# A VectorE shuffle for the pair swap of the rotary embedding, dummy products on TensorE, and units moved by tables

## The chip, the cores and the metric

One NeuronCore of a Trainium2 chip runs the kernel. The metric is the device time of one execution in microseconds (us), of which three were taken. The engines are TensorE (PE, with its weight loads apart as PEld), VectorE (DVE), ScalarE (ACT), GpSimd (POOL) and SyncE (SP), which issues most of the DMAs.

## The reference

The input `x` is (4, 1024, 256). It is normalised over its last axis, goes through a causal attention with 16 heads of 64 and through a mixture of 32 experts, and both results are added to `x`:

```python
xn = _layernorm(x)
q, k, v = (split_heads(xn @ W) for W in (Wq, Wk, Wv))
q, k = apply_rope(q), apply_rope(k)
attn = softmax(where(causal, q @ k.T * d**-0.5, -inf))
x = x + (attn @ v).merged @ Wo + bo + _L0_ffn_ref(xn, ...)
```

`apply_rope` turns neighbouring pairs of features. With `x1` the even and `x2` the odd feature, the even output is `x1*cos - x2*sin` and the odd one `x1*sin + x2*cos`. So every feature needs its neighbour's value. The expert part softmaxes gate logits over the tokens, takes the 8 best tokens per expert, merges them, runs two layers of 257x1024 and 1025x256 per expert, and adds the result back to those tokens.

## The kernel before, in words

All five engines run programs written out by hand, with semaphores between them. The work is a row of stages `(P, g)`: `P` is one of 32 steps (4 batches times 8 pairs of heads) and `g` is 0 to 5. Two stages `(-1, 4)` and `(-1, 5)` stand ahead of them. In stage `(P, g)` TensorE does, in this order:

- the scores of two key chunks of pair `P` (`scores`, L1448 to L1460), into the PSUM tiles `t_pA` and `t_pB`;
- the products from which the row maxima of pair `P + 1` are taken (`maximum`, L1472 and L1479), into `t_pC` and `t_pA`;
- one projection of a coming pair (`fill`), into the PSUM bank `t_pF`: q or k (L1525) at g = 0, 1, 4, 5, v (L1508) at g = 2, 3. A fill may start when the bank was read, that is when all earlier `cos_done` and `fill_read` are there;
- `turn_maxima` (L1536) at g = 1 and 4; then a `unit` of the opening, or slots of the expert layers, or output products;
- the products of the exponentials with v (`values`, L1550) into `t_pO`, and the sums (L1559).

A q or k fill is turned with features on the partitions, so a pair of features lies on two neighbouring partitions. Five steps follow it: ScalarE copies the bank to `t_raw` (`evict`, L861); SyncE issues two DMAs that copy even rows of `t_raw` to odd rows of `t_swap` and the reverse (L653, L622 for the first four); VectorE multiplies the bank with the cosines (`rope`, L1132, which also waits for `raw_done`); GpSimd multiplies `t_swap` with the sines (L737) and adds both (L740). Then ScalarE rounds the result to `t_HI` (`high`, L871) and VectorE takes the rest, `t_LO` (`low`, L1122). ScalarE may overwrite `t_raw` only when the DMAs of the last swap have landed:

```python
r = ROPE[f]
if r > EARLY:
    swap_ready(act, r - 1)
act.activation(raw_of(r), bank, ACT.Copy).then_inc(raw_done, 1)
```

Each engine goes through the stages with an order of its own. ScalarE: exponentials (L839), `high`, `evict`, weight rounding, units. VectorE: row maxima (`TENSOR_REDUCE`, L1098), `shift` (L1112), `low`, `combine` (L1105), `rope`, the reciprocal and normalisation of outputs (L1082, L1090), weight remainders (L1309), units, statistics. GpSimd: the `rope` of the stage before, then the additions of the exponentials into `t_acc` (L758 to L762).

In the opening (`P` up to 5) the batches 1 to 3 are made ready between the attention stages: `spread` (L1205) and `statistics` take sums, `variance(2)` and `moments(2)` make mean and scale of these batches, `normalise` on ScalarE (L934) applies them, the unit `x` transposes them (L1644), ScalarE and VectorE split them (L946, L1251), and the unit `logit` makes gate logits. The tables `STATISTICS_AT`, `NORM_AT` and `UNITS_AT` say in which stage each of these stands. A unit uses the upper banks of `t_pC` and `t_pB`, and the second score chunk of the next stage waits until VectorE has read them.

`warm(n)` (L1693) multiplies the identity with itself into `t_pO`, and nothing reads the result. It stands at two places before the first fill, with 16 and 4 products.

Of the kernel before, what the change touches and what calls it, by code (L numbers as in the profile page):

```python
# [30 lines left out]
P128 = 128  # L31
# [99 lines left out]
def parts_of(P, g):  # L131
# [4 lines left out]
UNITS_AT = {(0, 5): ("logit", 0), (1, 5): ("x", 1, 0), (2, 1): ("x", 1, 1), (2, 2): ("logit", 1), (2, 3): ("x", 2, 0),  # L136
            (3, 1): ("x", 2, 1), (3, 2): ("logit", 2), (3, 3): ("x", 3, 0), (4, 1): ("x", 3, 1), (4, 2): ("logit", 3),
# [4 lines left out]
STATISTICS_AT = {(0, 2): [(1, 0)], (0, 3): [(1, 1)], (0, 4): [(2, 0)], (0, 5): [(2, 1)], (1, 0): [(3, 0)], (1, 1): [(3, 1)]}  # L142
NORM_AT = {(1, 4): [(1, 0, (0, 1, 2, 3))], (1, 5): [(1, 1, (4, 5))], (2, 0): [(1, 1, (6, 7))], (2, 1): [(2, 0, (0, 1))],
           (2, 2): [(2, 0, (2, 3))], (2, 4): [(2, 1, (4, 5))], (2, 5): [(2, 1, (6, 7))], (3, 1): [(3, 0, (0, 1))],
           (3, 2): [(3, 0, (2, 3))], (3, 4): [(3, 1, (4, 5))], (3, 5): [(3, 1, (6, 7))]}
# [40 lines left out]
def attend_block(nc, x, wq, wk, wv, wo, bo, gate_w, gate_b, w1, w2, rot_cos, rot_sin, out):  # L186
# [17 lines left out]
    with ExitStack() as ctx:  # L204
# [64 lines left out]
        raw = sb("t_raw", [P128, BANK])  # L269
# [45 lines left out]
        def raw_of(r):  # L315
            return PT[:, r // 2, r % 2, :] if r < EARLY else raw[:, :]

# [18 lines left out]
        raw_done = sem("t_raw_done")  # L336
        swapped = [sem(f"t_swapped{i}") for i in range(2)]
# [35 lines left out]
        first_swapped = [sem(f"t_first_swapped{r}") for r in range(EARLY)]  # L373
# [107 lines left out]

        def swap_ready(engine, r):
            if r < EARLY:
                engine.wait_ge(first_swapped[r], 32)
            else:
                engine.wait_ge(swapped[r % 2], ((r - EARLY) // 2 + 1) * 32)
# [5 lines left out]
        def _(sp):  # L492
# [145 lines left out]
            for s, (P, g) in enumerate(STAGES):  # L638
# [91 lines left out]
        def _(pool):  # L730
            def rope(f):
# [4 lines left out]
                swap_ready(pool, r)  # L736
# [84 lines left out]
        def _(act):  # L821
            def exp(P, c, j):
# [5 lines left out]
                if n < PTS:  # L828
                    for r in range(2 * (n % 2), 2 * (n % 2) + 2):
                        if n < 2:  # L830
                            act.wait_ge(first_swapped[r], 32)
                        else:
                            act.wait_ge(first_turned[r], 1)
                else:
                    m = n - PTS
                    act.wait_ge(pv_done, m + 1)
                    P0, (c0, j0) = m // len(CHUNKS), CHUNKS[m % len(CHUNKS)]
                    act.wait_ge(acc_done, ACC_OPS[P0, c0, j0 if j0 else 1])
                act.activation(PT[:, n % PTS, :, 0:w], bank[:, :, 0:w], ACT.Exp, scale=SCALE).then_inc(exp_done, 1)  # L839

            def evict(f):

                n = FILL[f]
                bank = fill_bank(f)
                act.wait_ge(proj_done, n + 1)
                if f[0] == "v":
                    unit, t = f[1:]
                    if t < 4:
                        if unit >= 2:
                            act.wait_ge(pv_done, chunk_index(2 * unit - 3, 1, 3) + 1)  # L850
                        dst = V0[:, unit % 2, t:t + 2, :]
                    else:
                        if unit >= 1:
                            act.wait_ge(pv_done, chunk_index(2 * unit - 1, 1, 7) + 1)
                        dst = V1[:, t - 4:t - 2, :]
                    act.activation(dst, bank.rearrange("p (t n) -> p t n", t=2), ACT.Copy).then_inc(fill_read, 1)
                else:
                    r = ROPE[f]
                    if r > EARLY:
                        swap_ready(act, r - 1)  # L860
                    act.activation(raw_of(r), bank, ACT.Copy).then_inc(raw_done, 1)  # L861
# [140 lines left out]
            evict(("q", 0, 1))  # L1002
            evict(("k", 0, 1))
# [11 lines left out]
            for s, (P, g) in enumerate(STAGES):  # L1015
# [28 lines left out]
                if fill_of(P, g):  # L1044
                    evict(fill_of(P, g))
# [15 lines left out]
                if (P, g) == (1, 3):  # L1061
                    root(2)
# [15 lines left out]
        def _(dve):  # L1078
# [46 lines left out]
            def rope(f):  # L1125
# [166 lines left out]
            def first_sine(f):  # L1292
# [3 lines left out]
                swap_ready(dve, r)  # L1296
# [523 lines left out]
```

## Time and profile before

| what | value |
|---|---|
| median of 3 runs | 1391.26 us (1390.22 to 1393.01) |
| the profiled execution's own time | 1394.52 us |
| its span, first to last instruction | 1392.7 us |
| mean granted TensorE clock | 0.984 |
| TensorE matmul busy | 1326.8 us, 95% |
| VectorE busy | 876.9 us, 63% |
| ScalarE busy | 640.9 us, 46% |
| GpSimd busy | 976.6 us, 70% |
| moved by DMA | 188.88 MB |

An engine's busy time is a sum over stretches with different limits. Since TensorE stands at 95%, the table is read by its other 5%: 65.9 us of the span in which it ran nothing. The clock is a share of 2.4 GHz, and 0.50 in a stretch is the lower level of 1.2 GHz.

### The profile page before, as it was taken

To read this page: it belongs to the slowest core of one execution; us is meant where nothing else is said; L and a number is where in the kernel's file an instruction comes from. 1 tells how busy PE (TensorE), PEld (TensorE's weight loads), DVE (VectorE), ACT (ScalarE), POOL (GpSimd) and SP (SyncE) were. 2 spreads that over 40 slices of the span, in tenths; PEclk is the share of its full clock that TensorE was granted. 3 is DMA by queue.
4 is the path that set the end of the run, shared out by engine and by line. 5 is a ranking of instruction groups with operands and counts; after the bars stand their busy time and mean duration, and the time that the engine had idled before them with its cause. 6 is when DMAs were issued, how large, how long until landed. Compare 5 with 4: busy or idle time off the path is not lost.

```text
span 1392.7 us, 31589 instructions
## 1 busy us (share of the span) xinstructions
PE 1326.8 (95%) x11676; PEld 870.7 (63%) x11676; DVE 876.9 (63%) x1185; ACT 640.9 (46%) x969; POOL 976.6 (70%) x661
## 2 busy tenths in 40 slices
PE   6898999999899999999899999999999999999998
PEld 5565666655565555556667676666656776666656
DVE  5687667865555666556555666665757666665753
ACT  3445655543453344435433434544444434455542
POOL 2676667865665666558666777887879777888954
PEclk9898999999999999999999999999999999999999
DMA  5322333487678667774552221212232121222111
GB/s 179 116 73 86 140 138 123 169 287 249 221 257 298 217 219 240 270 245 154 150 167 77 89 85 62 78 63 78 92 108 89 63 77 62 77 66 81 61 58 62
DMA packets 122753, 188.88 MB, mean 136 GB/s; under 512 B 29616, under 2 KB 57808, under 8 KB 122608
## 3 DMA queue, kind: packets, MB, share of 16 engines
q1 hardware_dynamic: 92176, 112.51, 24.6%
q10 hardware_dynamic: 30384, 74.23, 15.5%
q8 instruction: 101, 1.65, 0.5%
q14 instruction: 44, 0.36, 0.1%
q0 software_dynamic: 48, 0.13, 0.1%
HBM read 130.71 MB, written 22.54 MB: 110 GB/s over the span
## 4 chain that ended last, share of the span: by engine, by line
PE 71%; DMA 10%; DVE 7%; POOL 3%; issue 3%; ACT 3%; SPq 2%; ACTq 0%; DVEq 0%; POOLq 0%
PE t_pO L1550 15%; PE t_pF L1525 11%; PE t_pA L1448 8%; PE t_pB L1448 6%; PE t_pF L1508 5%; DMA t_swap<-t_raw 4%; PE t_pA L1472 3%; PE t_pC L1472 3%; DMA r_s<-t_rcomp 2%; PE t_pC L1599 2%; PE t_pB L1599 2%; PE t_pA L1453 2%; PE t_pC L1559 2%; PE t_pB L1453 2%; POOL t_acc L762 2%
## 5 line engine op out<-in xcount | busy, mean ns | idle before, releaser
L762 POOL TENSOR_TENSOR t_acc<-t_acc,t_PT 128x1024 f32<-128x1024 f32 (+3 forms) x256 | 433.2, 1692 | 153.9 <-ACT t_PT L839 133.4
L737 POOL TENSOR_TENSOR t_swap<-t_swap,t_sin 128x512 f32<-128x512 f32 x124 | 169.9, 1370 | 199.8 <-DMA t_swap<-t_raw 198.3
L1550 PE MATMUL t_pO<-t_PT,t_V 128*64 128x512 f32 (+3 forms) x1536 | 292.0, 501 | 0.1
L839 ACT ACTIVATE t_PT<-t_pA 128x1024 f32<-128x1024 f32 x192 | 169.6, 883 | 260.0 <-PE t_pA L1460 226.0
L1525 PE MATMUL t_pF<-t_xT,t_wqk 128*128 128x512 f32 x756 | 215.1, 421 | 6.7 <-issue 3.9
L740 POOL TENSOR_TENSOR t_rot<-t_rot,t_swap 128x512 f32<-128x512 f32 x124 | 184.1, 1485 | 9.7
L1550 PEld LDWEIGHTS t_pO<-t_PT,t_V 128*64 128x64 f32 x1536 | 93.7, 137 | 139.8 <-issue 123.3
L861 ACT ACTIVATE t_raw<-t_pF 128x512 f32<-128x512 f32 x124 | 74.0, 597 | 195.5 <-PE t_pF L1525 135.3
L1525 PEld LDWEIGHTS t_pF<-t_xT,t_wqk 128*128 128x128 f32 x756 | 136.0, 193 | 43.8 <-issue 15.6
L1122 DVE TENSOR_TENSOR t_LO<-t_rot,t_HI 128x512 fp32r<-128x512 f32 x124 | 147.9, 1193 | 7.1 <-ACT t_HI L871 7.1
L839 ACT ACTIVATE t_PT<-t_pB 128x768 f32<-128x768 f32 (+1 forms) x192 | 141.9, 739 | 13.6 <-PE t_pB L1460 7.6
L1098 DVE TENSOR_REDUCE t_nm<-t_pC 128x2 f32<-128x256 f32 (+2 forms) x96 | 71.9, 777 | 119.8 <-PE t_pC L1479 119.8
L759 POOL TENSOR_TENSOR t_acc<-t_PT 128x768 f32<-128x768 f32 x64 | 139.2, 2175 | 6.9 <-ACT t_PT L839 6.8
L1098 DVE TENSOR_REDUCE t_nma<-t_pC 128x2 f32<-128x1024 f32 x66 | 80.9, 1225 | 77.3 <-PE t_pC L1472 77.2
L1132 DVE TENSOR_TENSOR t_rot<-t_pF,t_cos 128x512 f32<-128x512 f32 x124 | 85.3, 688 | 47.9 <-ACT t_raw L861 45.0
L1508 PE MATMUL t_pF<-t_wvs,t_xT 128*128 128x256 f32 x756 | 108.0, 293 | 4.1 <-issue 4.1
L1508 PEld LDWEIGHTS t_pF<-t_wvs,t_xT 128*128 128x128 f32 x756 | 95.3, 193 | 13.6 <-issue 12.3
L1448 PE MATMUL t_pA<-t_HI 64*128 64x512 f32 (+1 forms) x384 | 89.3, 462 | 6.9 <-DVE t_nma L1098 5.4
L1448 PEld LDWEIGHTS t_pA<-t_HI 64*128 64x128 f32 x384 | 36.0, 184 | 87.6 <-issue 77.2
L1448 PE MATMUL t_pB<-t_HI 64*128 64x512 f32 (+2 forms) x384 | 72.9, 375 | 12.9 <-DVE t_g L1148 7.8
L1472 PE MATMUL t_pA<-t_HI 64*128 64x512 f32 (+1 forms) x320 | 75.1, 465 | 9.4 <-ACT t_PT L839 8.7
L1472 PE MATMUL t_pC<-t_HI 64*128 64x512 f32 (+2 forms) x448 | 79.5, 374 | 3.8 <-ACT t_HI L871 1.8
(233 smaller groups left out, 2414.3 us busy)
## 6 DMA issues: line engine op xcount, KB each, us to landing
t_w1t<-in_L_ffn_w ACTq DMA_DIRECT2D x32, 1024.0 KB, 6.2
t_w2t<-in_L_ffn_w ACTq DMA_DIRECT2D x32, 1024.0 KB, 9.0
t_swap<-t_raw SPq DMA_DIRECT2D x248, 128.0 KB, 2.1
t_OT<-r_s SPq DMA_DIRECT2D x128, 128.0 KB, 3.0
t_wqk<-wqk_s SPq DMA_DIRECT2D x24, 512.0 KB, 3.7
xt_s<-t_xs SPq DMA_DIRECT2D x6, 1024.0 KB, 5.0
t_xT<-xt_s ACTq DMA_DIRECT2D x6, 1024.0 KB, 6.2
t_wvs<-wv_s SPq DMA_DIRECT2D x12, 512.0 KB, 5.0
```

Source lines behind the costliest of these rows:

```text
L737: pool.tensor_tensor(swap_of(r), swap_of(r), sin[:, c * BANK:(c + 1) * BANK], ALU.mult).then_inc(sin_sem, 1)
L740: pool.tensor_tensor(rot_of(r), rot_of(r), swap_of(r), ALU.add).then_inc(rot_sem, 1)
L759: pool.tensor_tensor(a[:, :, off:], first[:, :, off:], pt, ALU.add).then_inc(acc_done, 1)
L762: pool.tensor_tensor(a[:, :, off:], a[:, :, off:], pt, ALU.add).then_inc(acc_done, 1)
L839: act.activation(PT[:, n % PTS, :, 0:w], bank[:, :, 0:w], ACT.Exp, scale=SCALE).then_inc(exp_done, 1)
L1098: op = dve.tensor_reduce(dst, bank[:, :, at:at + w], AX_X, ALU.max, negate=True)
L1122: dve.tensor_tensor(LO[:, P % 2, z, q], rot_of(r), HI[:, P % 2, z, q].bitcast(F32), ALU.subtract).then_inc(lo_done, 1)
L1448: pe.matmul(bank[:, h, 0:w], hk[d, P % 2, 1, k], hq[d, P % 2, 0, q], start=(a == 0), stop=False)
L1472: mm = pe.matmul(bank[:, h, at:at + w], HI[d, pair % 2, 0, i * P128:(i + 1) * P128], HI[d, pair % 2, 1, k0:k0 + w], start=True, stop=not diag)
L1508: mm = pe.matmul(bank[:, u * 2 * P128:(u + 1) * 2 * P128], xT[:, c, hx, k, q], wvs[:, hw, k, :], start=(a == 0), stop=(a == 3 * KT - 1))
L1525: mm = pe.matmul(bank, wqk[:, hw, k, z * P128:(z + 1) * P128], xT[:, c, hx, k, :], start=(a == 0), stop=(a == 3 * KT - 1))
L1550: mm = pe.matmul(pO[h * DH:(h + 1) * DH, off:], v, PT[:, n % PTS, h, 0:w], start=(j == 0), stop=(j == 4 * c + 3))
```

## The change

- `evict` on ScalarE is left for v alone. The tile `t_raw`, its semaphore and the swap DMAs of SyncE go. In their place `rope` on VectorE begins with a `stream_shuffle` that reads the bank and writes `t_swap` with partitions 0 and 1, 2 and 3 and so on exchanged; the product with the cosines follows it.
- `warm` gets the bank as a parameter. The first call grows from 16 to 28 products, 8 stand in `(-1, 4)` behind the scores, and 6 each in `(0, 0)` and `(0, 1)` ahead of the fill.
- The statistics of the batches 1 to 3 stand one stage earlier each, `variance(2)` goes from `(1, 2)` to `(1, 1)`, `root(2)` and `moments(2)` from `(1, 3)` to `(1, 2)`. `normalise` (the table `NORM_AT`, not shown) stands one stage earlier with them, and the four row groups of (1, 1), which had two stages, come into one. Four units `x` move: (1, 0) from `(1, 5)` to `(1, 4)`, (1, 1) from `(2, 1)` to `(1, 5)`, (2, 1) from `(3, 1)` to `(2, 4)` and (3, 1) from `(4, 1)` to `(3, 4)`.

```diff
-UNITS_AT = {(0, 5): ("logit", 0), (1, 5): ("x", 1, 0), (2, 1): ("x", 1, 1), (2, 2): ("logit", 1), (2, 3): ("x", 2, 0),
-            (3, 1): ("x", 2, 1), (3, 2): ("logit", 2), (3, 3): ("x", 3, 0), (4, 1): ("x", 3, 1), (4, 2): ("logit", 3),
+UNITS_AT = {(0, 5): ("logit", 0), (1, 4): ("x", 1, 0), (1, 5): ("x", 1, 1), (2, 2): ("logit", 1), (2, 3): ("x", 2, 0),
+            (2, 4): ("x", 2, 1), (3, 2): ("logit", 2), (3, 3): ("x", 3, 0), (3, 4): ("x", 3, 1), (4, 2): ("logit", 3),
...
-STATISTICS_AT = {(0, 2): [(1, 0)], (0, 3): [(1, 1)], (0, 4): [(2, 0)], (0, 5): [(2, 1)], (1, 0): [(3, 0)], (1, 1): [(3, 1)]}
+STATISTICS_AT = {(0, 1): [(1, 0)], (0, 2): [(1, 1)], (0, 3): [(2, 0)], (0, 4): [(2, 1)], (0, 5): [(3, 0)], (1, 0): [(3, 1)]}
...
@@ sync: after every q or k fill
-                f = fill_of(P, g)
-                if f in ROPE:
-                    r = ROPE[f]
-                    sp.wait_ge(raw_done, r + 1)
-                    if r >= EARLY + 2:
-                        sp.wait_ge(sin_done, r - EARLY - 1)
-                    for o in range(2):
-                        sp.dma_start(swap[o::2, r % 2, :], raw[1 - o::2, :]).then_inc(swapped[r % 2], 16)
@@ gpsimd: rope
-                swap_ready(pool, r)
+                pool.wait_ge(swapped, r + 1)
@@ scalar: stage
-                if fill_of(P, g):
+                if fill_of(P, g) and fill_of(P, g)[0] == "v":
                     evict(fill_of(P, g))
@@ vector: rope
-                dve.wait_ge(raw_done, r + 1)
+                dve.wait_ge(proj_done, FILL[f] + 1)
                 if r >= EARLY + 2:
                     dve.wait_ge(lo_done, r - 1)
+                dve.stream_shuffle(swap_of(r), fill_bank(f), [i ^ 1 for i in range(32)]).then_inc(swapped, 1)
                 dve.tensor_tensor(rot_of(r), fill_bank(f), cos[:, c * BANK:(c + 1) * BANK], ALU.mult).then_inc(cos_done, 1)
@@ vector: stage
-                if (P, g) == (1, 2):
+                if (P, g) == (1, 1):
                     variance(2)
-                if (P, g) == (1, 3):
+                if (P, g) == (1, 2):
                     moments(2)
@@ tensor
-            warm(16)
+            warm(28, pO)
...
                     scores(*chunks[1])
+                    if (P, g) == (-1, 4):
+                        warm(8, pO)
...
+                if (P, g) in ((0, 0), (0, 1)):
+                    warm(6, pB[:, 1, :])
                 if fill_of(P, g) and not after_gelu:
                     fill(fill_of(P, g))
```

How the built programs differ at three places follows. A row is one or more instructions: line, operation, tile written and tiles read, shape of what is written.

TensorE in stages `(0, 0)` to `(0, 2)`, before the change:

```order
56 L1472 MATMUL t_pC<-t_HI 128x512 x2
57 L1472 MATMUL t_pA<-t_HI 128x512 x2
58 L1479 MATMUL t_pA<-t_maskq,t_maskd 128x64 x4
59 L1525 MATMUL t_pF<-t_xT,t_wqk 128x512 x12
60 L1536 MATMUL t_pB<-t_ident,t_nm 128x128
```

And of the change:

```order
57 L1429 MATMUL t_pC<-t_HI 128x512 x2
58 L1429 MATMUL t_pA<-t_HI 128x512 x2
59 L1436 MATMUL t_pA<-t_maskq,t_maskd 128x64 x4
60 L1650 MATMUL t_pB<-t_ident 128x128 x6
61 L1482 MATMUL t_pF<-t_xT,t_wqk 128x512 x6
62 L1650 MATMUL t_pB<-t_ident 128x128 x6
63 L1482 MATMUL t_pF<-t_xT,t_wqk 128x512 x6
64 L1493 MATMUL t_pB<-t_ident,t_nm 128x128
```

The two q and k fills of 6 products stood together; now 6 dummy products stand ahead of each.

VectorE in stages `(1, 2)` and `(1, 3)`, before the change (`t_ve` is the end of `variance(2)`, `t_r` and `t_nbias` are `moments(2)`):

```order
103 L1122 TENSOR_TENSOR t_LO<-t_rot,t_HI 128x512
104 L1082 RECIPROCAL t_rcomp<-t_comp 128x8
105 L1309 TENSOR_TENSOR t_wqk<-t_wraw,t_wqk 128x512
106 L1222 TENSOR_SCALAR t_mean<-t_both 128x24
107 L1223 TENSOR_TENSOR t_gap<-t_gap 128x24
108 L1224 TENSOR_SCALAR t_mse<-t_square 128x24
109 L1226 SCALAR_TENSOR_TENSOR t_ve<-t_gap,t_mse 128x24
110 L1098 TENSOR_REDUCE t_nm<-t_pC 128x2
111 L1098 TENSOR_REDUCE t_nma<-t_pA 128x2
```

And of the change:

```order
119 L1078 TENSOR_TENSOR t_LO<-t_rot,t_HI 128x512
120 L1038 RECIPROCAL t_rcomp<-t_comp 128x8
121 L1266 TENSOR_TENSOR t_wqk<-t_wraw,t_wqk 128x512
122 L1190 RECIPROCAL t_r<-t_sd 128x24
123 L1192 TENSOR_TENSOR t_r<-t_r 128x24
124 L1194 TENSOR_TENSOR t_r<-t_r,t_ve 128x24
125 L1196 TENSOR_SCALAR t_r<-t_r 128x24
126 L1198 TENSOR_TENSOR t_rstd<-t_r 128x24
127 L1200 SCALAR_TENSOR_TENSOR t_nbias<-t_mean,t_rstd 128x24
128 L1054 TENSOR_REDUCE t_nm<-t_pC 128x2
129 L1054 TENSOR_REDUCE t_nma<-t_pA 128x2
```

Four instructions ahead of the two maxima of `(1, 3)` have gone, and the six of `moments(2)`, each of which waits for the one before it, stand in their place.

## Rows read from the trace of the kernel before

**Rows 1.** The page: busy time, share of the span, instructions of each engine.

```profile
PE 1326.8 (95%) x11676; PEld 870.7 (63%) x11676; DVE 876.9 (63%) x1185; ACT 640.9 (46%) x969; POOL 976.6 (70%) x661
```

**Rows 2.** TensorE's waits: released by, us in total, times, longest.

```profile
PE t_pA L1472 <- ACT t_PT L839: 8.7, 4, 5.0
PE t_pB L1448 <- DVE t_g L1148: 7.8, 6, 3.5
...
PE t_pA L1448 <- DVE t_nma L1098: 5.4, 2, 3.6
...
PE t_pB L1448 <- DVE t_xs L1251: 3.4, 2, 1.8
```

**Rows 3.** Stretches at half clock: sum, busy PE, PEld, DVE, ACT, POOL, clock.

```profile
13.79:16.70 2.91, 2.90 (x14) 2.91 (x15) 1.76 (x4) 1.19 (x2) 0.00 (x0) 0.50 0.47 191
41.30:47.40 6.10, 6.10 (x16) 2.88 (x16) 2.75 (x4) 0.60 (x1) 0.43 (x1) 0.50 0.36 130
57.54:60.95 3.41, 3.41 (x9) 2.38 (x11) 0.62 (x2) 1.20 (x3) 1.49 (x2) 0.52 0.39 140
116.39:125.96 9.57, 9.57 (x49) 6.24 (x51) 5.01 (x12) 3.24 (x5) 4.16 (x2) 0.50 0.00 0
187.40:190.10 2.70, 2.70 (x26) 2.31 (x22) 0.36 (x2) 1.10 (x2) 2.56 (x3) 0.50 0.61 237
354.80:358.10 3.30, 3.30 (x11) 2.26 (x11) 0.62 (x5) 3.21 (x5) 2.89 (x3) 0.51 0.75 225
677.76:682.30 4.54, 4.54 (x23) 4.26 (x24) 3.35 (x6) 2.21 (x4) 4.32 (x4) 0.50 0.03 2
```

**Rows 4.** Groups by line: out<-in xcount | busy, mean ns | idle before, releaser.

```profile
L737 POOL TENSOR_TENSOR t_swap<-t_swap,t_sin 128x512 f32<-128x512 f32 x124 | 169.9, 1370 | 199.8 <-DMA t_swap<-t_raw 198.3
...
L1122 DVE TENSOR_TENSOR t_LO<-t_rot,t_HI 128x512 fp32r<-128x512 f32 x124 | 147.9, 1193 | 7.1 <-ACT t_HI L871 7.1
...
L1132 DVE TENSOR_TENSOR t_rot<-t_pF,t_cos 128x512 f32<-128x512 f32 x124 | 85.3, 688 | 47.9 <-ACT t_raw L861 45.0
```

**Rows 5.** The swap DMAs of L653, from issue to landing.

```profile
DMA to landing us min/median/max: 1.9/2.1/8.8
```

**Rows 6.** Timeline around 354 us, expert stretch: start, us, instruction, idle before.

```profile
354.04 0.33 PE L1448 MATMUL t_pB<-t_HI 64*128 64x128 f32 x2 [3.52 <-DVE t_g L1148]
...
352.37 0.69 DVE L1132 TENSOR_TENSOR t_rot<-t_pF,t_cos 128x512 f32<-128x512 f32 x1 [4.86 <-ACT t_raw L861]
...
351.74 0.60 ACT L861 ACTIVATE t_raw<-t_pF 128x512 f32<-128x512 f32 x1 [5.82 <-DMA t_swap<-t_raw]
```

**Rows 7.** Timeline around 676 us, where the output products begin.

```profile
677.76 0.69 PE L1472 MATMUL t_pA<-t_HI 64*128 64x384 f32 x2 [5.05 <-ACT t_PT L839]
...
674.77 0.60 ACT L861 ACTIVATE t_raw<-t_pF 128x512 f32<-128x512 f32 x1 [6.08 <-DMA t_swap<-t_raw]
```

**Rows 8.** TensorE in the opening: a window over dummy products, then its timeline.

```profile
5.50:7.70 2.20, 2.20 (x16) 1.00 1.19 350
...
13.79 1.97 PE L1683 MATMUL t_pA<-t_ident,t_xn 128*128 128x128 f32 x8 [6.09 <-ACT t_xn L934]
...
38.08 0.50 PE L1472 MATMUL t_pC<-t_HI 64*128 64x512 f32 x2 [1.39 <-ACT t_HI L871]
...
57.54 2.79 PE L1525 MATMUL t_pF<-t_xT,t_wqk 128*128 128x512 f32 x6 [3.05 <-issue]
```

**Rows 9.** Timeline around 110 us, ahead of the maxima of stage (1, 3).

```profile
111.78 2.28 DVE L1226 SCALAR_TENSOR_TENSOR t_ve<-t_gap,t_mse 128x24 f32<-128x24 f32 x1
...
108.87 5.15 POOL L762 TENSOR_TENSOR t_acc<-t_acc,t_PT 128x1024 f32<-128x1024 f32 x2
```

**Rows 10.** TensorE after the unit of stage (4, 1), by timeline.

```profile
228.88 0.50 PE L1448 MATMUL t_pB<-t_HI 64*128 64x512 f32 x2 [1.36 <-ACT t_PT L839]
```

**Rows 11.** One stage change: TensorE's fill, and VectorE's cosine product ahead of it.

```profile
943.95 1.69 PE L1508 MATMUL t_pF<-t_wvs,t_xT 128*128 128x256 f32 x12
...
942.65 0.69 DVE L1132 TENSOR_TENSOR t_rot<-t_pF,t_cos 128x512 f32<-128x512 f32 x1
```

More of the change, by code:

```diff
@@ L268, in attend_block @@
         wraw = sb("t_wraw", [P128, KT, 2 * P128])
-        raw = sb("t_raw", [P128, BANK])
         swap = sb("t_swap", [P128, 2, BANK])
@@ L313, in weights_raw @@
             return OC[:, n - 1, :].rearrange("p (k n) -> p k n", k=KT) if n in (1, 2) else wraw[:, :, :]
-        def raw_of(r):
-            return PT[:, r // 2, r % 2, :] if r < EARLY else raw[:, :]
         def swap_of(r):
@@ L335, in attend_block @@
         fill_read = sem("t_fill_read")
-        raw_done = sem("t_raw_done")
-        swapped = [sem(f"t_swapped{i}") for i in range(2)]
+        swapped = sem("t_swapped")
         cos_done = sem("t_cos_done")
@@ L372, in attend_block @@
         first_loaded = [sem(f"t_first_loaded{n}") for n in range(3)]
-        first_swapped = [sem(f"t_first_swapped{r}") for r in range(EARLY)]
         first_turned = [sem(f"t_first_turned{r}") for r in range(EARLY)]
@@ L480, in turns_before @@
             return 1 + sum((g == 1 and 0 <= P < N) + (g == 4 and 0 < P + 1 < N) for P, g in STAGES[:s])
[L482 to L486, printed above, removed]
         def nm_cols(a, n):
@@ L645, in _ @@
                     first_output()
-                f = fill_of(P, g)
-                if f in ROPE:
-                    r = ROPE[f]
-                    sp.wait_ge(raw_done, r + 1)
-                    if r >= EARLY + 2:
-                        sp.wait_ge(sin_done, r - EARLY - 1)
-                    for o in range(2):
-                        sp.dma_start(swap[o::2, r % 2, :], raw[1 - o::2, :]).then_inc(swapped[r % 2], 16)
                 n2 = normalise_of(*STAGES[s - 2]) if s >= 2 else None
@@ L828, in exp @@
                 if n < PTS:
[L829 to L833, printed above, removed]
+                    for r in range(2 * (n % 2), 2 * (n % 2) + 2) if n >= 2 else ():
+                        act.wait_ge(first_turned[r], 1)
                 else:
@@ L841, in evict @@
             def evict(f):
[L843 to L856, printed above, removed]
-                else:
[L858 to L861, printed above, removed]
+                act.wait_ge(proj_done, FILL[f] + 1)
+                unit, t = f[1:]
+                if t < 4:
+                    if unit >= 2:
+                        act.wait_ge(pv_done, chunk_index(2 * unit - 3, 1, 3) + 1)
+                    dst = V0[:, unit % 2, t:t + 2, :]
+                else:
+                    if unit >= 1:
+                        act.wait_ge(pv_done, chunk_index(2 * unit - 1, 1, 7) + 1)
+                    dst = V1[:, t - 4:t - 2, :]
+                act.activation(dst, fill_bank(f).rearrange("p (t n) -> p t n", t=2), ACT.Copy).then_inc(fill_read, 1)
             def high(f):
@@ L1001, in _ @@
             high(("q", 0, 0))
-            evict(("q", 0, 1))
-            evict(("k", 0, 1))
             evict(("v", 0, 2))
@@ L1295, in first_sine @@
                 c = f[2]
-                swap_ready(dve, r)
+                dve.wait_ge(swapped, r + 1)
                 dve.tensor_tensor(swap_of(r), swap_of(r), sin[:, c * BANK:(c + 1) * BANK], ALU.mult).then_inc(first_sin[r], 1)
@@ L1394, in _ @@
                     dve.tensor_tensor(gThl[:, 1, :, :, :], gT[:, :, :, :], gThl[:, 0, :, :, :].bitcast(F32), ALU.subtract).then_inc(g_lo, 1)
+                if (P, g) == (1, 1):
+                    variance(2)
                 if (P, g) == (1, 2):
-                    variance(2)
-                if (P, g) == (1, 3):
                     moments(2)
@@ L1689, in first_maximum, with warm @@
                 maximum(0, m, (pC, pA)[m % 2], FIRST_MAXIMA[m])
-            def warm(n):
+            def warm(n, bank):
                 for i in range(n):
-                    pe.matmul(pO[:, 0:P128], ident[:, :], ident[:, :], start=True, stop=True)
+                    pe.matmul(bank[:, 0:P128], ident[:, :], ident[:, :], start=True, stop=True)
             pe.wait_ge(ident_made, 2)
-            warm(16)
+            warm(28, pO)
             first_transposes(0)
-            warm(4)
+            warm(4, pO)
             fill(("k", 0, 0))
```

14 lines of the change are left out of this document (3 added, 11 removed).

## The prediction

> **What bounds the kernel now.** I began with the busy shares [rows 1]: TensorE 95%, no other engine over 70%. So TensorE's order of work sets the time, and only two things can be taken out: the 65.9 us in which it runs nothing (span 1392.7 less busy 1326.8), and work that it does at the lower clock. The table of its waits [rows 2] says who ends the idle time. The four largest causes are exponentials that come late (8.7 us), a gate product of VectorE in the expert layers (7.8), row maxima (5.4) and splits of a turned unit (3.4), 25.3 us together. The rest is small pieces that hang on no part of the change. The windows at half clock [rows 3] sum to 32.5 us of busy time at a granted 0.50, that is 1.2 GHz in place of 2.4, so some 16.3 us would be saved at 2.4. In each of them TensorE had waited just before.
>
> What makes it wait? By line [rows 4], GpSimd's product with the sines stands idle for 198.3 us behind the swap DMAs, and VectorE's cosine product 45.0 us behind ScalarE's copy. The DMAs mostly land 2.1 us after issue, but at worst 8.8 [rows 5]. What a late one does is seen at 351 us [rows 6]: ScalarE waited 5.82 us for the last swap before it could copy the bank; VectorE's cosine product, in order behind it, started 4.86 us late; the gate product of the expert layers stood behind that, and TensorE waited 3.52 us. At 674 us it is the same with the exponentials [rows 7]: ScalarE waited 6.08 us, its next exponential was late, TensorE waited 5.05 us.
>
> **The change, part by part.** Removed: 124 copies of 0.60 us on ScalarE [rows 6], and two DMAs for each. ScalarE is at 46%, so its 74 us are worth nothing by themselves; the DMAs are waited for only by GpSimd (70%) and ScalarE. What counts is that nobody waits for a DMA that can be 8.8 us late.
>
> Added: 128 shuffles on VectorE, 128x512 from the bank. No row shows one. The nearest is the cosine product, which reads the same bank at the same size in 0.69 [rows 4]; below it stands ScalarE's copy with 0.60, above it the product of two SBUF tiles with 1.19 (L1122). I take 0.69, and 88 us more work puts VectorE at 69%. The Trainium skill, "VectorE: DVE Perf Modes", section on the perf-mode tier table, gives the shuffle one speed only, some 2400 ns for 2048 elements. By it 512 would be estimated at 0.60, and no run here shows it yet.
>
> 1. *Expert stretch.* The waits for the gate product are 7.8 us in 6. Without the DMA ahead of the cosine product I leave one average wait of 1.3, so 6.5 go. The half-clock window at 354.8 follows such a wait; half of its 3.3, or 1.65, comes back. **-8.1** (bounds -2, if the next thing in order is late too, and -14, if all small idle pieces there go as well).
> 2. *677 us.* Of 5.05 some 0.5 stay, and half of 4.54 comes back: 4.55 + 2.27. **-6.8** (bounds -2 and -9).
> 3. *Opening, dummy products.* One costs 0.275: 16 records, two for each, in 2.20 us at full clock [rows 8]. Eight (2.2 us) behind the scores of `(-1, 4)` lie partly in the wait of 1.39 at 38.08 us and for the rest in the idle pieces behind it, and no work of TensorE's is due there. If they hold the clock, half of 6.1 comes back: -3.05. In `(0, 0)` and `(0, 1)` there is a wait of 3.05 at 57.54, then 3.41 at half clock (1.7 lost). The twelve products take 3.3 of the 4.75, which leaves -1.45. The twelve more of the start lie in the 6.09 before 13.79 and cost nothing: 3.3 is under 6.09. The idle time left, 2.8, is near the 3.05 behind which the clock fell, so I count a quarter of the 1.45 lost there: -0.4. **-4.9** (bounds -1, dummies that don't hold the clock, and -8).
> 4. *Stages (0, 3) and (0, 4).* The smaller wait for maxima, 5.4 less 3.6, or 1.8 [rows 2], grows: sums of the statistics come a stage earlier, and two shuffles of 0.69 stand ahead. **+1.4** (0 to +3).
> 5. *Stage (1, 3).* The wait of 3.6 for maxima and 9.57 at half clock behind it (4.8 lost) are the costliest place. Of the four small products of `variance(2)` one took 2.28 us beside two additions of GpSimd [rows 9]. They leave, and six dependent ones take their place. **-1** (-8.4 if the stall goes with its clock, +5 if it grows: GpSimd's pair of additions takes 5.15).
> 6. *Units.* The splits of second halves were waited for twice (3.4) [rows 2], and the third cost 1.36 behind 228.88 [rows 10]. The half clock from 187.4 is 1.35. All of this goes with their stages: -6.15. At the new places the same splits come due before a second score chunk. First halves, which stand at such places, show no row; I take 1.1 for each of three, two thirds of the old mean. **-2.85** (-6 to +2).
> 7. *Everything else*, 32 pairs. **0**, because the shuffle stands in the place of ScalarE's copy in the chain from a fill to the next one: where VectorE waited for the copy (45.0 us) the copy is gone, and where it came late it has the slack of the change to the next fill, 0.61 us at the least seen of those I took out [rows 11], mostly 1.0 to 1.4. (-1 to +10.)
>
> Sum: -8.1 - 6.8 - 4.9 + 1.4 - 1 - 2.85 = -22.3. The profiled execution took 1394.52; less 22.3 it would be 1372.3. It stands 3.26 above the median of 1391.26, so the median comes to 1369.0.
>
> *A rule against the change.* The cosine product stayed at 0.69 throughout, while L1122, with two SBUF inputs, had a mean of 1.19 [rows 4] with GpSimd at work for 70% of the time. The Trainium skill, "SBUF — State Buffer", section "Who interferes with whom", says the same of the two: with two SBUF inputs VectorE and a reading GpSimd block each other for a whole instruction, and with at most one they don't. By it the shuffle, which reads only PSUM, is safe and term 7 stands, but the six products of term 5 can each be blocked.
>
> **Rivals.**
> A. *The stalls only move on.* Terms 1 and 2 come to nothing, since late work of VectorE (gates of the expert layers, now with more ahead) takes the DMA's place. For it: VectorE goes to 69%. Against: in [rows 6, 7] every engine's lateness leads back to the DMA. -22.3 + 14.9 = -7.4: 1383.9.
> B. *The moments are blocked.* The six products take the length of GpSimd's two additions (5.15) and the stall of term 5 grows by up to 5 with its low clock kept: -22.3 + 1 + 4: 1374. [Rows 9] bear it out for one product. It is the case that the rule cited from the Trainium skill, "SBUF — State Buffer", would bring about.
> C. *Slower.* The shuffle costs c, and the bank comes free later at the two tight changes of each pair by c less a slack of some 1.1. It eats the gain when 64 (c - 1.1) = 22.3, so from c = 1.45. At 1.8, 64 x 0.7 = 44.8 and the time is 1413.8. Against: the cosine product of the same bank takes 0.69; only L1122 comes near.
> D. *Nothing.* The dummies don't hold the clock and the swap was hidden everywhere: 1391.
>
> **How the numbers follow.** Forecast 0.62, A 0.18, B 0.08, C 0.08, D 0.04. The range leaves out C (0.08), D (0.04) and some 0.08 of the forecast's own tails. Its upper end, 1387, is A with some loss in term 7; its lower end, 1355, is the forecast with two thirds of what the good bounds of terms 1, 2, 3, 5 and 6 add (5.9 + 2.2 + 3.1 + 7.4 + 3.15 = 21.8; two thirds are 14.5). A measurement of this kernel tells about 0.2%, 2.8 us, from no change. Faster is the forecast, A and B less 0.02 for A's poor end: 0.86. Same is D and a little of A: 0.05. Slower is C and the rest: 0.09.
>
> **What would show it.** Right: no wait for DMAs on ScalarE or GpSimd's sines; the shuffle at 0.6 to 0.7 x128; TensorE's waits for the gate product under 2 us; windows at 41, 57, 354 and 677 us at a clock of 1.00; TensorE's idle time near 50. Wrong: a shuffle over 1.2; waits of TensorE's fills for the cosine product in every pair (term 7, C); new waits for exponentials or gates in place of the old (A); a wait for maxima over 5 us near 116 us (B).

## The result, and the profile after

The change took the kernel from a median of 1390.22 us (7 runs, 1382.17 to 1393.01) to 1379.72 us (7 runs, 1375.40 to 1385.35). The ratio is 0.9928 with a 95% interval of 0.9905 to 0.9951, so it is faster by 0.7%. The forecast was 1369.0, or 1.6%. The time lies in the stated range, but the size was over twice what came.

The page after, in the rows that answer to [rows 1] and [rows 4]: busy time, then groups by line (columns as ahead of the prediction).

```profile
span 1378.2 us, 31345 instructions
...
PE 1325.2 (96%) x11740; PEld 871.7 (63%) x11740; DVE 958.5 (70%) x1441; ACT 567.9 (41%) x841; POOL 970.7 (70%) x661
...
L708 POOL TENSOR_TENSOR t_swap<-t_swap,t_sin 128x512 f32<-128x512 f32 x124 | 167.6, 1352 | 100.0 <-DVE t_swap L1088 100.0
...
L1078 DVE TENSOR_TENSOR t_LO<-t_rot,t_HI 128x512 fp32r<-128x512 f32 x124 | 164.2, 1324 | 7.6 <-ACT t_HI L831 7.5
...
L1088 DVE STREAM_SHUFFLE t_swap<-t_pF 128x512 f32<-128x512 f32 x124 | 91.8, 740 | 0.8 <-issue 0.4
...
L1089 DVE TENSOR_TENSOR t_rot<-t_pF,t_cos 128x512 f32<-128x512 f32 x124 | 83.6, 674 | 0.0
```

The shuffle takes 0.74 us, near the 0.69 that was taken. ScalarE lost 73 us, VectorE gained 82, and GpSimd waits 100 us less for the swap. The remainder product (`low`, L1078, L1122 before) went from 1.193 to 1.324 us. TensorE's idle time went from 65.9 to 53.0 us.

TensorE's waits after: released by, us in total, times, longest. They answer to [rows 2].

```profile
PE t_pF L1465 <- issue: 9.9, 20, 0.6
PE t_pB L1405 <- DVE t_g L1105: 5.0, 9, 0.9
...
PE t_pB L1493 <- ACT t_PT L807: 3.9, 3, 1.9
PE t_pB L1405 <- ACT t_PT L807: 3.1, 3, 1.1
PE t_pA L1410 <- DVE t_D L1068: 2.7, 2, 1.8
...
PE t_pF L1482 <- issue: 2.3, 12, 0.2
```

The waits of 5.0 and 3.6 us are gone, and no single wait beyond the start is over 1.9. What stands on top now is "issue" ahead of a fill (L1465 is v, L1482 q and k), the wait for the bank `t_pF` to be read: 12.2 us in 32 waits, all short. Before, there were 8 such waits with 8.0 us, of which the one at 57.54 [rows 8] had 3.05, and only one of them stood behind 860 us. The clock has changed with the long waits. These windows of after (columns: window, its length, TensorE busy, clock, DMA share, GB/s) answer to [rows 3], at the same places of the program:

```profile
43.30:47.40 4.10, 4.10 (x32) 1.00 0.76 231
55.00:59.00 4.00, 3.89 (x26) 1.00 0.00 0
96.00:106.00 10.00, 8.19 (x61) 0.83 0.30 106
106.00:112.00 6.00, 5.45 (x46) 1.00 0.16 48
178.00:182.00 4.00, 3.76 (x45) 1.00 0.67 246
342.00:347.00 5.00, 4.66 (x41) 1.00 1.00 348
657.00:663.00 6.00, 5.06 (x54) 1.00 0.56 141
```

**Where the time went.** TensorE runs its 189 fills of `t_pF` in the same order in both kernels, so the two traces can be laid side by side: the start of a fill after, less its start before. Where this difference falls, the change gains; where it rises, it loses.

| up to fill (its start before, us) | difference | step | forecast for it |
|---|---|---|---|
| 7 (63.70) | -2.92 | -2.9 | term 3: -4.9 |
| 12 (97.16) | -2.91 | 0.0 | term 4: +1.4 |
| 18 (140.23) | -4.41 | -1.5 | term 5: -1 |
| 36 (263.23) | -8.65 | -4.2 | term 6: -2.85 |
| 86 (641.93) | -15.01 | -6.4 | term 1: -8.1 |
| 98 (748.55) | -23.34 | -8.3 | term 2: -6.8 |
| 188 (1322.63) | -13.97 | +9.4 | term 7: 0 |

At fill 98 the change is 23.3 us ahead; the six terms up to there had forecast 22.25. Then it gives 9.4 back, in a part of the program that the forecast had at nothing. Most of the loss has one shape. This is after, at the stage change of [rows 11], from TensorE and from VectorE:

```profile
924.83 0.36 PE L1465 MATMUL t_pF<-t_wvs,t_xT 128*128 128x256 f32 x1 [0.41 <-issue]
...
921.47 1.82 DVE L1078 TENSOR_TENSOR t_LO<-t_rot,t_HI 128x512 fp32r<-128x512 f32 x1
923.40 0.01 DVE L1088 LOAD_MASK_SELECT t_swap<-t_pF  x1
923.42 0.74 DVE L1088 STREAM_SHUFFLE t_swap<-t_pF 128x512 f32<-128x512 f32 x1
924.05 0.68 DVE L1089 TENSOR_TENSOR t_rot<-t_pF,t_cos 128x512 f32<-128x512 f32 x1
```

The cosine product ends at 924.73 and the fill that waits for its bank starts at 924.83. Ahead of it VectorE did the remainder (1.82 us beside GpSimd) and the shuffle (0.63 from its start to the next). Before, the product ended 0.61 us ahead of the fill.

### The profile page after: what moved, and what is told of

It reads as the page before. It is cut to its first block, busy times and chain, and to the rows that moved or that the text cites. A ratio compares the mean times of both kernels' runs of the same rounds, so it can differ in the third digit from the quotient of the medians.

```text
span 1378.2 us, 31345 instructions
## 1 busy us (share of the span) xinstructions
PE 1325.2 (96%) x11740; PEld 871.7 (63%) x11740; DVE 958.5 (70%) x1441; ACT 567.9 (41%) x841; POOL 970.7 (70%) x661
## 4 chain that ended last, share of the span: by engine, by line
PE 82%; DVE 10%; DMA 3%; issue 3%; ACT 2%; SPq 0%; ACTq 0%; POOL 0%; DVEq 0%; POOLq 0%
PE t_pO L1507 17%; PE t_pF L1482 12%; PE t_pA L1405 9%; PE t_pB L1405 7%; PE t_pF L1465 7%; PE t_pA L1429 3%; PE t_pC L1429 3%; PE t_pC L1556 3%; PE t_pA L1410 2%; PE t_pB L1556 2%; PE t_pB L1410 2%; PE t_pC L1516 2%; DVE t_LO L1078 1%; DVE t_OT L1046 1%; DVE t_nma L1054 1%
## 5 line engine op out<-in xcount | busy, mean ns | idle before, releaser
L1482 PE MATMUL t_pF<-t_xT,t_wqk 128*128 128x512 f32 x756 | 209.8, 413 | 5.5 <-issue 2.3
L711 POOL TENSOR_TENSOR t_rot<-t_rot,t_swap 128x512 f32<-128x512 f32 x124 | 180.2, 1453 | 9.7
L1078 DVE TENSOR_TENSOR t_LO<-t_rot,t_HI 128x512 fp32r<-128x512 f32 x124 | 164.2, 1324 | 7.6 <-ACT t_HI L831 7.5
L1482 PEld LDWEIGHTS t_pF<-t_xT,t_wqk 128*128 128x128 f32 x756 | 133.4, 189 | 41.3 <-issue 15.0
L1465 PE MATMUL t_pF<-t_wvs,t_xT 128*128 128x256 f32 x756 | 106.6, 290 | 10.0 <-issue 9.9
L1465 PEld LDWEIGHTS t_pF<-t_wvs,t_xT 128*128 128x128 f32 x756 | 94.3, 191 | 20.2 <-issue 19.6
L848 ACT ACTIVATE t_srow<-t_pC 128x256 f32<-128x256 f32 x64 | 24.6, 384 | 184.1 <-PE t_pC L1516 184.1
L841 ACT ACTIVATE t_OC<-t_pO 128x512 f32<-128x512 f32 x64 | 38.3, 598 | 145.3 <-PE t_pO L1507 145.1
L1405 PE MATMUL t_pA<-t_HI 64*128 64x512 f32 (+1 forms) x384 | 88.6, 458 | 4.3 <-DVE t_nmb L1054 2.5
L1088 DVE STREAM_SHUFFLE t_swap<-t_pF 128x512 f32<-128x512 f32 x124 | 91.8, 740 | 0.8 <-issue 0.4
L1054 DVE TENSOR_REDUCE t_nmb<-t_pC 128x2 f32<-128x256 f32 (+1 forms) x62 | 31.7, 553 | 87.0 <-PE t_pC L1436 87.0
```

The lines of the kernel that those rows point to most:

```text
L711: pool.tensor_tensor(rot_of(r), rot_of(r), swap_of(r), ALU.add).then_inc(rot_sem, 1)
L1054: op = dve.tensor_reduce(dst, bank[:, :, at:at + w], AX_X, ALU.max, negate=True)
L1078: dve.tensor_tensor(LO[:, P % 2, z, q], rot_of(r), HI[:, P % 2, z, q].bitcast(F32), ALU.subtract).then_inc(lo_done, 1)
L1088: dve.stream_shuffle(swap_of(r), fill_bank(f), [i ^ 1 for i in range(32)]).then_inc(swapped, 1)
L1405: pe.matmul(bank[:, h, 0:w], hk[d, P % 2, 1, k], hq[d, P % 2, 0, q], start=(a == 0), stop=False)
L1465: mm = pe.matmul(bank[:, u * 2 * P128:(u + 1) * 2 * P128], xT[:, c, hx, k, q], wvs[:, hw, k, :], start=(a == 0), stop=(a == 3 * KT - 1))
```

## The experiments

Each ratio is against runs of the kernel before on the same chip. A trace is one execution, and all differences at a fill are against the first trace of before, if nothing else is said. Theory 1 says that the loss comes from the bank, which VectorE now frees later; theory 2, at first, that it comes from VectorE's load wherever it stands.

**Which part gains.** Five kernels take the change apart.

```diff
 # shuffle alone: after, less
-            warm(28, pO)
+            warm(16, pO)
-                        warm(8, pO)
-                    warm(6, pB[:, 1, :])
 # and UNITS_AT, STATISTICS_AT, NORM_AT, variance, moments, root as before
```

> The shuffle alone: no new dummy products, tables as before. Theory 1 (the DMA stalls go, but the shuffle frees the bank later at the two tight stage changes of each pair): read from the two traces, the stretch 300 to 641 us gains 6, 677 to 731 gains 9, the tight changes of pairs give back 0.65 each and other places some 1 us, 9.4 in the second half: about -6 us against before, most of the forecast's terms 1 and 2 and a cost that the forecast had at nothing. Waits of TensorE's fills for the bank (shown as issue) about 12 us in 30 or more. Theory 2 (the gain of after is from the opening alone): 0 or slower than before.

Measured: 1393.50 us, ratio 1.0035 (1.0010 to 1.0060), slower than before. The second half was as expected (+0.25 and +0.43 at the two fills of each steady pair, +8.0 us from fill 98 to 188), and so was the gain ahead of it (from +5.1 at fill 36 to -8.4 at fill 98). What the expectation missed is that the difference at fill 36 is +5.1. Its waits say where most of it is (columns as above):

```profile
PE t_pF L1465 <- issue: 9.5, 19, 0.7
PE t_pB L1405 <- DVE t_xs L1208: 7.9, 3, 3.1
```

The splits of the units (`t_xs`) are waited for 7.9 us in place of 3.4 [rows 2]: VectorE has a shuffle more ahead of them. So the shuffle without the tables makes the opening worse.

The dummy products alone on the kernel before:

```diff
-            warm(16)
+            warm(28, pO)
+                    if (P, g) == (-1, 4):
+                        warm(8, pO)
+                if (P, g) in ((0, 0), (0, 1)):
+                    warm(6, pB[:, 1, :])
```

> The dummy products alone on the kernel before: the clock is held at 41 to 47 us and at 57 us, -2.9 us (where the two traces stand apart by 60 us). Rival: with the swap by DMA the idle time of the opening is longer than the dummies and the clock falls all the same: 0.

Measured: 1388.21 us, ratio 0.9996 (0.9967 to 1.0026). Nothing can be told; 2.9 us would be 0.2% and lie inside the interval. The trace has the step of -2.5 at fill 4 that after has too, but is only 1.6 us ahead at fill 7, and the second trace of before, below, is 1.7 us ahead there without a dummy more.

The tables alone on the kernel before (the first hunks of the diff, with `variance(2)` in (1, 1), `root(2)` and `moments(2)` in (1, 2)):

> The tables (statistics, normalise, units) alone on the kernel before: if they carry what after gained between 60 and 265 us, about -5.8 us. Rival: the gain there is that of the shuffle (splits and maxima come earlier because VectorE no longer waits for ScalarE's copy): -2 or less in size.

Measured: 1389.69 us, ratio 0.9994 (0.9969 to 1.0019): nothing either. Its trace stands at -8.7 at fill 36, as after does, and the medians don't show it. The second trace of before, below, explains this.

After with the tables of before, and after without the new dummies:

> After with the tables of before. Between fills 7 and 40 after gains 6 us on before, the shuffle alone loses 3.5: so with the shuffle the tables should be worth 10 us here, about 1390. Rival: the tables are worth what they measured alone on the kernel before, which is nothing: 1380.

> After without the new dummy products. At the sixth and seventh fill after stands at -1.5 to -2.9 us against before and the shuffle alone at +1.6: so the dummies are worth 3 to 4 us of the opening in after, and this kernel should take about 1383. Rival: the clock is held without them, 1380.

Measured: 1388.25 us, ratio 0.9984 (0.9969 to 0.9999), and 1386.89 us, ratio 0.9971 (0.9947 to 0.9995). Against the 1.0035 of the shuffle alone, the dummies are worth 0.5%, the tables 0.6%, and both together 1.1%, so the two add up. On the kernel before each measured as nothing, but the intervals allow 0.3% there, so it isn't shown that they are worth more beside the shuffle. For the tables the traces have a reason: the waits for splits are 7.9 us in the kernel with shuffle and dummies too, and after has none in its table. The first expectation (1390) held, the second was 4 us low.

**What the loss is.** In the next kernel ScalarE copies the bank again and the shuffle reads the copy, behind the cosine product. VectorE has the same work, but the bank is free as early as before.

```diff
-                dve.wait_ge(proj_done, FILL[f] + 1)
+                dve.wait_ge(raw_done, r + 1)
...
-                dve.stream_shuffle(swap_of(r), fill_bank(f), ...).then_inc(swapped, 1)
                 dve.tensor_tensor(rot_of(r), fill_bank(f), cos[...], ALU.mult).then_inc(cos_done, 1)
+                dve.stream_shuffle(swap_of(r), raw_of(r), ...).then_inc(swapped, 1)
... # evict of q and k, t_raw and raw_done as before
```

> After, but ScalarE copies the bank again and the shuffle reads that copy in SBUF, behind the cosine product: VectorE has the same work, the bank is free as early as before, and there is no DMA. Theory 1 (the loss is the bank): the 9.4 us of the second half come back, about 1370 us. Theory 2 (the loss is VectorE's load, whatever it reads): as after, 1380. The shuffle itself: 0.6 to 0.75 us if reading SBUF costs what PSUM does.

Measured: 1373.39 us, ratio 0.9878 (0.9843 to 0.9913). By the ratios it is 0.5% better than after, some 7 us, and its trace ends 9.6 us ahead of after's. The loss is gone: from fill 98 to 188 the difference goes from -21.26 to -23.56. The waits for the bank have left its table, of which these are the first rows:

```profile
PE t_pF L1502 <- DMA t_wqk<-wqk_s: 8.5, 7, 2.3
PE t_pC L1556 <- ACT t_PT L815: 4.4, 8, 0.6
```

The first row, fills that wait for a weight's DMA, is new (1.2 us in after), and no run explains it. The shuffle from SBUF takes the same:

```profile
L1109 DVE STREAM_SHUFFLE t_swap<-t_raw 128x512 f32<-128x512 f32 x124 | 91.2, 736 | 0.0
```

So VectorE's shuffles cost nothing in this half where they stand behind the bank's last read, and theory 2 falls for it. The opposite test doubles the shuffle, ahead of the cosine product:

```diff
+                if f[1] >= 2:
+                    dve.stream_shuffle(extra[:, :], fill_bank(f), ...)
                 dve.stream_shuffle(swap_of(r), fill_bank(f), ...).then_inc(swapped, 1)
```

> After with every shuffle from pair 2 on done twice (0.63 us more from start to start each), the first into a tile that nothing reads. Theory 1: at the two changes without slack each pair pays the full 0.63 twice, 1.26 a pair and some 35 us in 28 pairs, with more changes becoming tight: 1410 to 1425. Theory 2 (bank is free in time, the load is spread): under 10 us, 1390.

Measured: 1433.41 us in one run, above the range of theory 1. In the steady pairs the steps are +0.16, +0.85 and +1.06 at three fills, 2.1 us a pair where after has 0.7: the two tight changes pay nearly the whole 0.63 more, and a third one becomes tight. That is theory 1, but it is the smaller part. At fill 98 this kernel stands at +13.3 where after has -23.3, so 36.7 of the 53.7 us were lost ahead of it. The waits for gates and splits in its table say that VectorE's load counts there:

```profile
PE t_pF L1468 <- issue: 24.6, 23, 1.3
PE t_pF L1485 <- issue: 11.5, 17, 0.8
PE t_pB L1408 <- DVE t_g L1108: 11.4, 9, 2.3
PE t_pB L1408 <- DVE t_xs L1211: 7.8, 4, 2.3
```

**A better order.** The remainder stands ahead of the shuffle because two buffers of `t_rot` demand it. With a third one the order can be turned.

```diff
-        rot = sb("t_rot", [P128, 2, BANK])
+        rot = sb("t_rot", [P128, 3, BANK])
...
                 if r >= EARLY + 2:
-                    dve.wait_ge(lo_done, r - 1)
+                    dve.wait_ge(rot_done, r - EARLY - 1)
+                if r >= EARLY + 3:
+                    dve.wait_ge(lo_done, r - 2)
...
-                if f in ROPE:
-                    low(f)
...
                     rope(fill_of(P, g))
+                if f in ROPE:
+                    low(f)
```

> After with three buffers for the turned product in place of two, and VectorE takes the shuffle and the cosine product ahead of the remainder (low) of the fill two stages before, which in after stands ahead of them and takes up to 1.8 us beside GpSimd. Theory 1 (the loss is the late freeing of the bank at the tight changes): the waits of fills for the bank go, -9 us against after, about 1370, like the kernel with the copy kept. Theory 2 (VectorE's load, late remainders): same as after or worse, 1380 or more, since the load is the same and remainders come later. If TensorE's scores wait for a late remainder, it is this way that fails.

Measured: 1383.91 us, ratio 0.9956 (0.9933 to 0.9979). By the total, the rival was right; by the stages, both were. In the steady pairs the steps are 0.00 and 0.01, so the bank is no longer waited for. But in the expert layers the gate products now come later, and at the batch changes of pairs 16 and 24 the steps are +4.4 and +3.6 in place of 2.0 and 2.3:

```profile
PE t_pB L1407 <- DVE t_g L1107: 12.5, 9, 1.4
PE t_pB L1495 <- ACT t_PT L807: 6.2, 3, 3.0
```

It was the scores' second chunk and the turns that failed, not the scores' wait for a remainder. So the turned order belongs only where the bank is what is waited for (against after, with the three buffers of the kernel above):

```diff
+                ahead = P >= 17 and P % PAIRS != 0 and g < 2
...
-                if f in ROPE:
+                if f in ROPE and not ahead:
                     low(f)
...
                     rope(fill_of(P, g))
+                if f in ROPE and ahead:
+                    low(f)
```

> The three buffers of the rope-first kernel, but the shuffle and the cosine product go ahead of the remainder only at g = 0 and 1 of pairs from 17 on, without the pairs that begin a batch; elsewhere the order of after. Theory 1 (the loss of the steady pairs is the late bank, and the rope-first kernel lost elsewhere, by gate products and remainders that came later): about 9 us less than after, near 1371. Rival (three buffers or the order bring a loss of their own in the steady pairs): 1380.

Measured: **1367.60 us**, ratio 0.9842 (0.9809 to 0.9876). It has the lowest ratio of all, but the interval of the kernel with the copy kept (0.9843 to 0.9913) overlaps it. From fill 98 to 188 the difference goes from -23.24 to -22.61. Its waits for the bank all stand ahead of 620 us, where the order is that of after:

```profile
PE t_pF L1470 <- issue: 3.5, 8, 0.4
```

**The dummies of the first pair.** After without the six and six:

> After without the six and six products in (0, 0) and (0, 1), the others kept. If they hold the clock at the fill of (0, 1) and cost less than the wait there, TensorE stands 1 to 1.5 us later than in after from the eighth fill on. Rival (they fill time that would be idle and nothing else): the same.

Measured: 1381.07 us in one run. At fill 7 it stands at -1.24 against before where after has -2.92. Of these 1.7 us, 0.5 were there at fill 4 already, ahead of the six and six, so they are worth 1.2, as expected. Later differences between the two traces are larger than this and come from elsewhere, so only the step is used.

**How much of a trace is this execution alone.**

> The kernel before, unchanged, for a second trace. If terms 1, 2 and 5 of the prediction were sized on stalls that every execution has, the waits of 3.5 at 354, 5.0 at 677 and 3.6 at 116 us stand here too. If they come from where DMAs happened to land, some are missing or elsewhere, and the sum of the idle time is other than 65.9.

Measured: 1391.99 us, idle time 61.6 (span 1390.2 less busy 1328.6). These rows are its timeline at the places of [rows 6], [rows 7] and [rows 3]:

```profile
110.63 0.50 PE L1448 MATMUL t_pA<-t_HI 64*128 64x512 f32 x2 [1.41 <-DVE t_nma L1098]
...
345.36 0.33 PE L1448 MATMUL t_pB<-t_HI 64*128 64x128 f32 x2 [2.60 <-DVE t_g L1148]
...
619.90 0.48 PE L1448 MATMUL t_pB<-t_HI 64*128 64x128 f32 x2 [2.81 <-DVE t_g L1148]
673.97 0.69 PE L1472 MATMUL t_pA<-t_HI 64*128 64x384 f32 x2 [5.73 <-ACT t_PT L839]
```

The waits at 354 and 677 us are here too (2.60 and 5.73, with one of 2.81 that the first trace had not). The wait of 3.56 at 116 us is not: it is 1.41, and by fill 16 this execution is 10 us ahead of the first one, 6.5 of it in two steps at fills 15 and 16. The kernel with the dummies alone has the same two steps (-5.6 and -2.0). So the costliest place of the opening in the first trace was one that some executions don't have. By fill 98 that lead had shrunk to 3.2 us.

## Why the prediction was off

- **What bounds the kernel**: right. The removed DMA was the cause of the long waits at 354 and 677 us. ScalarE and GpSimd wait for no swap any more, and the windows at 354 and 677 us run at 1.00.
- **Term 1 (expert stretch)** -6.4 for -8.1. A wait of 0.51 for the gates stays in each pair where 1.3 in all was left, and a wait of 0.65 for the bank stands at eight v fills, 5.2 us (before: 4.1 us at six). **Term 2 (677 us)** -8.3 for -6.8: the wait and its clock gave 5.5, and a wait of 2.70 for one more late exponential at 719 us, with a clock of 0.63 over the 4.6 us behind it, gave 3.6, partly spent by other steps. There ScalarE had stood 6.03 us behind another DMA (`t_ol<-o_s`) and not behind a swap; after waits for the same DMA, but its exponential is only 0.65 late. Rival A, that they only move on, was wrong.
- **Term 3 (dummies)** -2.9 for -4.9. What failed here is less the dummies than a shuffle that no term had. At fill 7 the two kernels with the shuffle and without new dummies stand at +1.6 and +1.5, the one with the shuffle, the dummies and the tables of before at -2.4. So the dummies gave 3.9 us, and the shuffle took 1.5. VectorE's shift in stage (-1, 4) starts at 36.11 us where before it started at 34.52, behind one more shuffle and a product with the sines of 1.71 us in place of 0.69, and fill 3 comes 1.4 later. It comes 1.7 later in the kernel without new dummies and 0.0 later with the dummies alone, so the eight delay nothing. The clock that they hold gave 2.5 at fill 4 (0.3 without them). The first six do delay the next fill, by 1.3, and the clock gives that back and 1.2 more. The price of 0.275 held (12 records, six products, took 1.50 us at 54.46, so 0.25). The 0.7 that after is ahead at the first fill is of its trace alone: six of the seven other kernels with 28 products at the start stand between -0.04 and +0.07 there.
- **Terms 4 to 6** 0.0, -1.5 and -4.2 for +1.4, -1 and -2.85. They rest on the first trace of before, which held the stall at 116 us; measured against the second trace the opening as a whole gained nothing (-8.65 against -9.97 at fill 36). The tables alone at 0.9994 agree with that. In term 5 a wait of 1.81 for the shift at 99.54 came in, with a clock of 0.83 over 96 to 106 us. The six moments took 0.18 to 0.30 us each, but GpSimd was idle from 106.0 to 110.3 while they ran, so rival B did not happen and its mechanism was not put to the test. By the condition that the prediction states for it, two SBUF inputs, only four of the six could have been blocked, since L1190 and L1196 have one. Two readings were inexact, with no effect on the result: of the products of `variance(2)` two took over 2 us, L1222 with 2.37 as well, and what term 6 adds up to 6.15 is 6.11.
- **Term 7 (the steady pairs)** +9.4 for 0. This is the step that failed. The shuffle was rightly priced, but the sentence "where it came late it has the slack of the change to the next fill" was spent on the shuffle alone. Before, the ten steady pairs from 860 us on had a slack of 0.44 to 1.40 us at the two tight changes, 1.0 and 1.1 on average (0.61 was not the least), and most of them had room for 0.63. What the prediction left out is that the remainder ahead of the shuffle grows. Before it took 0.68 to 1.05 us at the first of the two changes and 0.68 to 1.47 at the second; after it takes 1.95 to 1.97 and 1.79 to 1.82 in every pair, since GpSimd no longer waits for a DMA and adds at the same time (read from the overlap: at 915.60 the remainder starts beside an addition of 915.20 to 917.02). Two kernels have only one of the two ahead of the bank's last read. With the copy kept it is the long remainder (1.95 and 1.37), a slack of 0.50 and 0.71 us is left, and nothing is lost. With the turned order it is the shuffle, and nothing is lost either. Only both together overrun the slack. Nine pairs lose 0.25 + 0.44 each, 6.2 us. Two batch changes lose 2.0 and 2.3 in another way, below. Places where before had stalls of its own give back 1.1. The bounds of this term (-1 to +10) held the value. Rival C named the very bank and was dismissed because it asked for a shuffle of 1.45 us. Its slack of 1.1 was right on average; what it lacked is the remainder's 0.9 to 1.1 us more.
- **The parts by their medians.** The forecast had -14.9 us for the shuffle (terms 1, 2 and 7) and -7.4 for dummies and tables. The shuffle alone measured 1.0035, some 5 us slower, and dummies and tables brought 1.1% on top of it, some 15 us. Terms 1 and 2 came: its trace gains 13.5 from fill 36 to 98. But the zero of term 7 hid 8.0 behind fill 98, and it hid a loss in the opening, where this kernel stands at +5.1 against the first trace of before and at +15.1 against the second. The shuffle's part was off by some 20 us and the other part by some 8 the other way (each interval is 3 to 4 us to either side), and that the total missed by only 12 is luck.
- **From the trace to the median.** The steps end at -14.0 and the span at -14.5, the medians 10.5 apart. The profiled execution of before was 4.3 above the median of its seven runs, that of after 0.3 above its own. I subtracted the sum from the offset execution and carried the offset of 3.26 on as it was; but part of it was stalls (the 116 us one) that the sum had already removed. That would account for the other 4 us. Against the second trace of before the steps are +1.3 up to fill 36, -21.5 up to 98 and +9.6 up to 188, together -10.5, which is the distance of the medians. But these are single traces of a kernel whose seven runs lie up to 10.8 us apart, so the agreement can be chance.

The batch change at pair 24 in full, from the trace of after (TensorE, VectorE, ScalarE, in order of time):

```profile
1058.06 1.43 DVE L1046 TENSOR_TENSOR t_OT<-t_OT,t_OC 128x512 f32<-128x512 f32 x1
...
1059.59 1.06 ACT L872 ACTIVATE t_oh<-t_OT 128x1024 fp32r<-128x1024 f32 x1 [6.04 <-DVE t_OT L1046]
...
1061.29 0.39 ACT L807 ACTIVATE t_PT<-t_pB 128x256 f32<-128x256 f32 x1
...
1061.73 0.33 PE L1493 MATMUL t_pB<-t_ident,t_nm 128*128 128x128 f32 x1 [1.86 <-ACT t_PT L807]
```

The normalisation of an output (L1046) stands behind the shuffle on VectorE. ScalarE's rounding waits for it, the exponential stands behind the rounding, and TensorE's turn waits 1.86 us for that. What follows runs at the lower clock. The same instructions before, first, and after (columns as in [rows 3]):

```profile
1080.49:1084.23 3.74, 3.74 (x27) 3.30 (x28) 2.38 (x4) 1.90 (x3) 3.60 (x3) 1.00 0.23 77
```
```profile
1061.73:1066.96 5.23, 5.23 (x28) 4.79 (x28) 3.00 (x6) 1.41 (x2) 5.01 (x5) 0.67 0.02 2
```

That is 0.89 us of longer wait and 1.49 us of slower products: 2.4 for a step of 2.3. No run changed this chain alone, but two bear on it. In the kernel with the copy kept the same normalisation takes 0.68 us in place of 1.43, the turn waits 1.29, the clock stays at 1.00, and the step is 0.3. And the lower clock does not always come. The last kernel above has the wait of 1.85 at both batch changes; here are the products behind it at pair 16 and at pair 24 (columns as in [rows 3]):

```profile
754.27:758.01 3.74, 3.74 (x27) 3.30 (x28) 2.92 (x6) 1.41 (x2) 3.60 (x4) 1.00 0.02 2
1056.30:1061.54 5.24, 5.24 (x28) 4.80 (x28) 2.89 (x6) 1.41 (x2) 5.02 (x5) 0.67 0.02 2
```

Seven kernels have a wait of 1.84 to 1.87 us at these two places, 14 in all. The clock fell behind seven of them and stayed at 1.00 behind the other seven, among them both of the kernel without the six and six, whose program is that of after in this half. Where it stayed, the batch change cost 0.5 at pair 16 and 0.9 at pair 24. So some 3 of the 9.4 us of term 7 are a lower clock that another execution may not have.

## What to carry to other kernels

Moving work to an engine with idle time is priced by what stands behind it: ask which buffer that instruction now holds, and set the slack of the tightest stage change, not a typical one, against everything in series ahead of it. And ask whether what stands in series ahead of it keeps its length: here it grew by more than the shuffle took. In the second half the shuffles cost 9 us ahead of the bank's last read and nothing behind it. When a term rests on a stall of one traced execution, take a second trace of the unchanged kernel first, and don't carry the execution's distance from the median past the terms that remove its stalls.

## What was not expected of the hardware

- The products behind a wait of 1.84 to 1.87 us of TensorE ran at a granted clock of 0.67 in seven cases and of 1.00 in seven, with the same instructions; in after it was 0.67 at both places. The lower clock cost 1.49 us (5.23 for 3.74). Behind the waits of 0.93 to 1.30 us at these places it was 1.00 in all ten, behind the two of 3.01 us 0.51 and 0.67. So one trace doesn't tell what such a wait costs.
- `stream_shuffle` of 128x512 takes 0.74 us from PSUM and 0.736 from SBUF, and 0.63 from its start to the next one's. Each brings a mask load of 0.01 us. The Trainium skill, "VectorE: DVE Perf Modes", section on the perf-mode tier table, gives some 2400 ns for 2048 elements, from which 0.60 was estimated. The trace has a quarter more in duration and 5% more from start to start.
- A neighbour became slower when GpSimd stopped waiting: the remainder with its two SBUF inputs rose from 1.193 to 1.324 us on average while its shape and count stayed, and the cosine product (0.688 and 0.674) did not. The four traces with the swap DMAs have 1.193 to 1.232, eight of the nine with the shuffle 1.314 to 1.348, and the ninth, with the order turned in the steady pairs only, 1.223. The Trainium skill, "SBUF — State Buffer", section "Who interferes with whom", tells the two apart in just this way, and the trace agrees.
